# First transfers of a persistent LoRA kernel on two queues: SyncE's list reordered, ScalarE issues some transfers, TensorE multiplies zeros first

## The reference

```
w = weights[conditions]                       # [64, 128, 128]
x = x + einsum('bct,bcd->bdt', x, w)          # first layer
H = einsum('btd,od->bto', x, W)               # W is 1024 x 1024
xa = einsum('btd,brd->btr', x, A[adapter])    # rank 16
delta = einsum('btr,bor->bto', xa, B[adapter]) * s[adapter]
out = x + H + delta                           # second layer
```

## Time and profile before

| | us |
|---|---|
| median of 3 runs | 772.71 (772.51 to 773.09) |
| the profiled execution | 773.48 |
| its span, first to last instruction | 771.7 |
| outside the span | 1.8 |
| PE busy / DVE busy / ACT busy / POOL busy | 760.3 / 613.8 / 503.9 / 190.1 |

### The profile page before, as it was taken

One profiled execution on the slowest core, in us unless ns is written; L12 is line 12 of the kernel. 1 busy time (PEld: TensorE's weight loads), 2 busy tenths in 40 slices (PEclk: granted clock), 3 DMA queues, 4 the chain that ended last, 5 costly groups with the idle time before them and its releaser, 6 DMA issues.

```text
span 771.7 us, 16748 instructions
## 1 busy us (share of the span) xinstructions
PE 760.3 (99%) x4418; PEld 719.3 (93%) x4418; DVE 613.8 (80%) x1386; ACT 503.9 (65%) x1173; POOL 190.1 (25%) x428
## 2 busy tenths in 40 slices
PE   7999999999999999999999999999999999999998
PEld 4567999999999999999999999999999999999997
DVE  5999977788777788777788777788777788777774
ACT  3476666676666676666676666676666676666673
POOL 2733202233212333202332212323212232212200
PEclk9999999999999999999999999999999999999999
DMA  8433343432343432333432343432343432343222
GB/s 288 169 131 116 124 144 123 151 120 90 122 143 122 150 117 94 122 143 122 150 118 92 122 143 122 150 112 98 122 143 122 150 117 94 122 143 122 89 90 83
DMA packets 47291, 98.32 MB, mean 127 GB/s; under 512 B 6438, under 2 KB 25894, under 8 KB 47270
## 3 DMA queue, kind: packets, MB, share of 16 engines
q1 hardware_dynamic: 47266, 98.08, 37.4%
q10 hardware_dynamic: 4, 0.00, 0.0%
HBM read 63.45 MB, written 34.60 MB: 127 GB/s over the span
## 4 chain that ended last, share of the span: by engine, by line
PE 87%; DVE 3%; DMA 1%; issue 1%; ACT 0%; SPq 0%; DVEq 0%; ACTq 0%
PE bank L1381 73%; PE o_ps L1442 4%; PE bank L1420 3%; PE o_ps L1441 3%; PE o_ps L1443 3%; DMA out<-o_sb 1%; DVE c_sb L892 1%; DVE w_lo L889 1%; DVE z_lo L889 0%; DVE x_lo L889 0%; PE bank L1425 0%; PE o_ps L1432 0%; DVE x_raw L889 0%; ACT x_hi L510 0%; ACT z_hi L510 0%
## 5 line engine op out<-in xcount | busy, mean ns | idle before, releaser
L1381 PE MATMUL bank<-w_hi,x_hi 128*128 128x342 f32 (+2 forms) x1200 | 390.5, 325 | 0.7 <-ACT c_sb L510 0.6
L1381 PE MATMUL bank<-w_lo,x_hi 128*128 128x342 f32 (+2 forms) x1200 | 387.1, 323 | 0.0
L1381 PE MATMUL bank<-w_hi,x_lo 128*128 128x342 f32 (+2 forms) x1200 | 386.5, 322 | 0.0
L1381 PEld LDWEIGHTS bank<-w_hi,x_hi 128*128 128x128 f32 x1200 | 225.8, 188 | 9.8 <-ACT c_sb L510 2.1
L1381 PEld LDWEIGHTS bank<-w_lo,x_hi 128*128 128x128 f32 x1200 | 225.6, 188 | 2.8
L1381 PEld LDWEIGHTS bank<-w_hi,x_lo 128*128 128x128 f32 x1200 | 226.1, 188 | 0.0
L889 DVE TENSOR_TENSOR x_lo<-x_raw,x_hi 128x256 fp32r<-128x256 f32 (+1 forms) x270 | 145.5, 547 | 32.0 <-ACT x_hi L510 27.3
L510 ACT ACTIVATE x_hi<-x_raw 128x256 fp32r<-128x256 f32 (+1 forms) x270 | 133.7, 507 | 52.5 <-PE bank L1381 45.7
L303 POOL TENSOR_TENSOR w_lo<-a_ride,w_hi 128x160 fp32r<-128x160 f32 x30 | 15.6, 519 | 507.0 <-ACT w_hi L510 507.0
L510 ACT ACTIVATE c_sb<-bank 128x342 f32<-128x342 f32 x190 | 85.7, 452 | 41.0 <-PE bank L1381 38.6
L510 ACT ACTIVATE z_hi<-c_sb 128x340 fp32r<-128x340 f32 (+1 forms) x128 | 60.4, 490 | 54.8 <-DVE c_sb L892 54.8
(11 more groups left out here) (104 smaller groups left out, 878.2 us busy)
## 6 DMA issues: line engine op xcount, KB each, us to landing
x_raw<-xT SPq DMA_DIRECT2D x62, 512.0 KB, 4.9
out<-o_sb SPq DMA_DIRECT2D x62, 512.0 KB, 2.7
b_stack_raw<-b_split SPq DMA_DIRECT2D x128, 128.0 KB, 2.4
a_now<-lora_a SPq DMA_DIRECT2D x64, 64.0 KB, 3.4
c_raw<-cond_w SPq DMA_DIRECT2D x64, 64.0 KB, 1.8
w_lo_raw<-wB SPq DMA_DIRECT2D x7, 342.0 KB, 7.5
w_hi_raw<-wB SPq DMA_DIRECT2D x5, 342.0 KB, 6.0
x_raw<-xT SPq DMA_DIRECT2D x4, 256.0 KB, 4.7
```

The costliest lines, as they stand in the source:

```text
L1381: last = nc.tensor.matmul(bank[:, lo:hi], x[:, left, c * C:(c + 1) * C], w[:, c, FIRST[o]:FIRST[o] + WIDTH[o]], start=opens and c == 0 and ...
```

## The change

On ACT's queue, ahead of the adapter numbers and the scales, stand now the two first halves of x of pair 0; SP's queue begins with `b12`, and the second halves of x come later in it. ACT, and no longer SP, reads the adapter numbers of pair 0 and starts its two A transfers, behind its first rounding (`hi_of("17")`). In SP's list the condition matrices of pair 0 (`load_c(0, 0, 0)`, with its wait and its two register reads) move ahead of the two saves of `b_split`, and the stack of pair 0 (`load_b(0, 0, 0)`, behind the wait for the saves) moves ahead of A of pair 1 (`load_a(sp, 0, 0, 1)`). TensorE gets 9 + 4 matmuls of zeros, 128 columns each, around the matmul of the scales; nothing reads their result. `load_a`, `load_x_half` and `adapters` become functions of the engine that issues.

```
+            load_x_half(act, 0, 0, x_half_landed[0])
+            load_x_half(act, 1, 0, x_half_landed[1])
             act.dma_start(adapter_sb[:, :], adapter_idx).then_inc(adapter_landed, 16)
             act.dma_start(s_row[:, :], scalings).then_inc(s_landed, 16)
...
             hi_of("17", w_block("b12"))
+            act.wait_ge(adapter_landed, 16)
+            load_a(act, 0, 0, 0)
...
-            load_x_half(0, 0, x_half_landed[0])
             load_w(sp, "b12")
-            load_x_half(1, 0, x_half_landed[1])
             load_w(sp, "b01")
-            load_x_half(0, 1, x_landed[0][0])
-            load_x_half(1, 1, x_landed[0][1])
             load_w(sp, "b30")
+            load_x_half(sp, 0, 1, x_landed[0][0])
             load_w(sp, "b21")
-            sp.wait_ge(adapter_landed, 16)
-            load_a(0, 0, 0)
+            load_x_half(sp, 1, 1, x_landed[0][1])
             load_w(sp, "b20")
...
             load_x(0, 0, 1, 1)
+            sp.wait_ge(cond_landed, 16)
+            load_c(0, 0, 0)
             sp.wait_ge(b_hi_ready, 1)
             save_b(0, z_hi[0])
+            sp.wait_ge(adapter_landed, 16)
             sp.wait_ge(b_lo_ready, 1)
             save_b(1, z_lo[0])
-            sp.wait_ge(first_scaled, 8)
-            load_a(0, 0, 1)
-            sp.wait_ge(cond_landed, 16)
-            load_c(0, 0, 0)
             sp.wait_ge(b_saved, 32)
             load_b(0, 0, 0)
+            sp.wait_ge(first_scaled, 8)
+            load_a(sp, 0, 0, 1)
             step(0, 0)
...
+            pe.wait_ge(zeros_ready, 1)
+            for _ in range(9):
+                nc.tensor.matmul(o_ps[1][:, 0:P], xa_cols[0][:, :], xa_cols[0][:, :], start=True, stop=True)
+
             pe.wait_ge(s_landed, 16)
             pe.wait_ge(ones_ready, 1)
             nc.tensor.matmul(o_ps[0][:, 0:NAD], ones[0:1, :], s_row[0:1, :], start=True, stop=True).then_inc(s_spread, 1)
+            for _ in range(4):
+                nc.tensor.matmul(o_ps[1][:, 0:P], xa_cols[0][:, :], xa_cols[0][:, :], start=True, stop=True)
             dense("b12")
```

More of the change, by code:

```diff
@@ L307, in o_last, with load_x_half @@
             return x_raw[0][:, n, 2 * h:2 * h + 2, :].rearrange("p k c -> p (k c)")
+        def load_x_half(eng, n, h, landed_sem):
+            eng.dma_start(x_raw[0][:, n, 2 * h:2 * h + 2, :].rearrange("p k c -> p (k c)"),
+                          xT[n, :, h * (KC // 2):(h + 1) * (KC // 2), :].rearrange("p k c -> p (k c)"))\
+               .then_inc(landed_sem, 16)
         def load_w(eng, b):
@@ L311, in load_w, with adapters, load_a @@
             eng.dma_start(w_block(b), wB[k, j, :, :, :]).then_inc(w_landed[b], 16)
+        def adapters(eng, i, j, d):
+            b = i * 4 + 2 * (j + d)
+            return [eng.value_load(adapter_sb[0:1, bass.ds(b + n, 1)], min_val=0, max_val=NAD - 1) for n in range(2)]
+        def load_a(eng, i, j, d):
+            found = adapters(eng, i, j, d)
+            after(eng, a_summed, i, j, d - 1, 4)
+            for n in range(2):
+                eng.dma_start(a_now[:, n, :, :].rearrange("p k r -> p (k r)"),
+                              lora_a[bass.ds(found[n], 1), :, :, :].rearrange("a p k r -> (a p) (k r)"))\
+                   .then_inc(a_landed, 16)
         @block.sync
@@ L319, in load_x @@
                              xT[bass.ds(b, 1), :, :, :].rearrange("b p k c -> (b p) (k c)")).then_inc(x_landed[s][n], 16)
[L321 to L331, removed]
             def load_b(i, j, d):
-                found = adapters(i, j, d)
+                found = adapters(sp, i, j, d)
                 after(sp, lora_done["00"], i, j, d - 1)
@@ L370, in step @@
                 if exists(i, j, 2):
-                    load_a(i, j, 2)
+                    load_a(sp, i, j, 2)
                 if exists(i, j, -1):
@@ L416, in _ @@
             store(0, 1, -1, 1)
-            load_a(0, 1, 2)
+            load_a(sp, 0, 1, 2)
             store(0, 1, -1, 0)
```

## The result

The changed kernel takes 776.56 us (median of 7 runs, 775.72 to 782.54). The kernel before, beside it on the same chip, takes 773.09 (772.51 to 773.37, 7 runs). The ratio is 1.0058, 95% interval 1.0040 to 1.0075: slower by 3.5 us. The forecast was 776.8, range 773.2 to 780.2.

The account below looks back on a forecast made before the run. The prediction took TensorE, busy 760.3 of 771.7 us, as the bound, with losses nearly all before pair 2. A 5.4 us lateness from the rides less 1.3 won back gave +4.1, 776.8 us, range 773.2 to 780.2.

Parts of the forecast that it names:

- Zeros first: TensorE's start: zero matmuls delay `b12` but at the higher clock; gain 0.4 to loss 1.9 us, hidden, counted 0.
- Two queues: Start of the weight stream: fuller DMA engines bring the weights 0.7 us sooner (bounds 0 and 1.5), by itself no time.
- A of pair 0: ScalarE's issue of A: landed at 13, hidden by POOL's later wait of 4.39 us; counted 0, at most 0.5.
- The saves: SP's saves of `b_split` behind the condition numbers: reached at 24.4, saved at 31.3 against 29.6 before; bounds 28.1 and 33.
- the bound of 7.7 us: Late bound for the condition numbers' landing: 7.7 us from issue, as x of pair 1 behind them took, giving 22.9.
- late bound of 33: Latest time at which the saves of `b_split` would be done and SP go on, against the 31.3 taken.
- The stack: Stack of pair 0 behind the saves: ready at 37.8 against 36.07, TensorE 1.7 us late at the adapter matmuls.
- The rides: POOL's copies for product "5" of pair 1: A landed at 39.2, ready 6.9 us later at 46.1, TensorE 5.4 us late.
- The rival of the clock: TensorE's clock falls in the wait before product "5": 2.3 us more, 779.1 us; chance 0.21.
- The 1.3 us won back: TensorE's two later waits, 0.7 and 0.6 us, would absorb 1.3 us of its lateness.
- The sum: Whole kernel: 5.4 us of lateness less 1.3 won back, +4.1 us, median from 772.71 to 776.8.

Follow-up runs that it names:

- no_zeros: saves_as_before without the 9 + 4 matmuls of zeros; 773.62 us, ratio 1.0001 to the kernel before.
- saves_as_before: The changed kernel with the tail of SP's list (saves, A of pair 1, condition matrices, stack) in the order of before; 773.42 us, ratio 1.0003.
- a_early_saves_late: The changed kernel with A of pair 1 fetched ahead of the wait for the saves, the saves still behind the condition matrices; 776.83 us, ratio 1.0053.
- store_first: saves_as_before with the store of the second sample moved ahead of the next x in each step; 772.02 us, ratio 0.9985.
- busy_in_the_wait: The changed kernel with nine 128-column float32 matmuls that nothing reads ahead of the wait for `b_stack`; 776.36 us, ratio 1.0042.
- saves_early_a_late: The changed kernel with the condition matrices put behind the saves again, A of pair 1 still last; 773.62 us, ratio 1.0000.
- again: The changed kernel measured and profiled once more, with no edit; 777.91 us, ratio 1.0052.

## Why the prediction came out near, step by step

**Zeros first: right in effect, late in time.** Forecast for `b12`: start 7.5 to 8.3, end 9.9 to 10.7. It started at 8.57 and the next block at 11.76, 3.19 us later and not 2.4. In four of the nine profiles with zeros it came as forecast: start at 7.7 to 7.9, 2.47 us for the 8 halves; in the other five they took 3.3 to 4.5. Worth nothing either way, as no_zeros shows (4.20 us for the 8 halves, the same time), because A of pair 0 takes the gain.

**Two queues: the start was undersized.** Forecast: 0.7 us sooner. SP issued the condition numbers at 11.55, 3.6 us before the 15.19 of the earlier trace rows: two halves of x, the wait for the adapter numbers, two reads and two issues of A had also left SP's list, which the prediction did not follow down the queue. For pairs 0 and 1 that gave "5" 1.1 us sooner (saves_as_before), and in the end nothing.

**A of pair 0: 14.5 and not 13, and not hidden.** In the nine profiles in which ScalarE issues it, TensorE waits for its scaling in five, 0.5 to 2.5 us at about 16 us: in the four in which the first block took 2.47 us, and in no_zeros. In the other four, in which the zeros had left that block slow, there is none. Either way the next block with 358 columns starts at 20.9 to 21.6 (saves_as_before 20.91, the changed kernel 21.17), but for 22.7 in a_early_saves_late and 24.1 in store_first. So the two terms, each put at nothing, hide each other.

**The saves: two errors that cancel.** SP came to them at 21.9 and not at 24.4, but went on at 31.6, as forecast (31.3). From the first issue to SP's next step it took 9.7 us where 6.9 were allowed. The prediction priced the saves at 205 GB/s from their first moment; that is what they reach in the end, not at the start. Before, behind x of pair 1, the stretches from 23 to 27 read 205 to 238 GB/s; why the start is slow here, no run shows:

```profile
24.00:25.00 1.00, 1.00 (x5) 0.64 (x4) 1.00 (x3) 0.42 (x1) 0.59 (x1) 1.00 0.45 49
...
27.00:28.00 1.00, 1.00 (x5) 0.61 (x4) 1.00 (x3) 1.00 (x2) 0.00 (x0) 1.00 0.50 205
```

The order of landing is as the bound of 7.7 us had it. The Trainium skill ("DMA: Bandwidth & Descriptors", section "Queues, rings and completion order") says that a semaphore's increment lands behind the earlier writes; 7.9 us for 256 bytes agrees. The DMA share is near half in both rows. The same page, section "Why a DMA increments its semaphore by 16 and not by 1", says that as many of the 16 engines are used as divide the slowest dimension; it is 8 here, and 0.50 agrees. (The prediction's late bound of 33 for this term is not the sum of the terms that it names: 22.9, 1.33, 0.86, 5.1 and 1.8 make 32.0.)

**The stack: right.** Forecast 1.7 us late at the adapter matmuls; 2.2 by the timeline (38.37 against 36.21). This, which the prediction counted as part of a longer wait, is the main loss: "5" starts at 42.67 in busy_in_the_wait, 2.0 late, with nothing else against it.

**The rides: the step that failed.** "POOL began the rides of pair 1 at 30.19 when A landed and ended its second copy at 37.07, 6.9 us" was carried over as the price, and with it "the rides are ready at 46.1". A landed at 38.7, near the forecast of 39.2; the copies ended at 42.5. No wait for them is in any profile. One instruction of the chain, in the trace of before:

```profile
34.53 0.76 POOL L299 TENSOR_TENSOR a_ride<-a_now,a_ride 128x32 f32<-128x32 f32 x1
```

In the changed kernel it is the row at 41.56: 0.25 us. Before, VectorE worked through that microsecond (1.00 in the stretch from 34 to 35) on L1152, with two tiles in SBUF as operands; in the changed kernel it had stopped at 41.4, since it too waited for TensorE. In saves_early_a_late the chain slows and quickens within one execution: the last of its 5.7 us fall in VectorE's pause from 37.8 to 39.3, and L299 takes 0.25 there. A busy VectorE alone is not what counts: in the trace of before L299 takes 0.25 us again at 73.04, beside VectorE's `z_lo<-bank,z_hi`, which reads one operand from a bank of PSUM, and 0.81 at 189.76 beside its `x_lo<-x_raw,x_hi`, two tiles in SBUF. The Trainium skill ("GPSIMD Engine Reference", section "2. Architecture") says that GpSimd reads and writes SBUF through ports that it shares with VectorE; the rows agree, though no run here stops VectorE and nothing else. The prediction's own bounds for this term, 6.6 to 7.5, came from one execution with VectorE at work, though it had written that VectorE's splits would wait behind TensorE. Over the profiles the chain takes 3.7 to 8.3 us (8.2 in saves_as_before).

**The rival of the clock: it occurs, at another wait.** It was given 0.21 and 2.3 us. The fall comes behind the wait for `b_stack`, of 2.3 to 4.7 us, in part of the executions, and costs 1.6 us to "5" in again and 3.2 in the profile of the changed kernel (44.27 and 45.82 against 42.67). In the profiles it goes with the length of the wait: every one of 2.3 to 4.7 us has a fall with it, none of 1.4 us or less has. The profile of the changed kernel shows a second one at 99 us:

```profile
85.72 7.73 DMA out<-o_sb
...
101.40 0.85 PE bank L1421 x3
```

```profile
100.00:101.00 1.00, 1.00 (x5) 1.00 (x5) 1.00 (x4) 0.52 (x2) 0.78 (x4) 0.50 0.00 0
```

The store took 7.73 us where the earlier trace rows have 5.87, TensorE waited 2.5 us for what hangs on it, and fell to half speed again. The Trainium skill ("TensorE: Matmul & The Clock Gate", section "HAM oscillation — how this bites in real kernels") says that a wait for a transfer brings the clock down; the granted clock here agrees.

**The 1.3 us won back: wrong.** The two later waits stayed (0.7 and 0.6 in again) or grew. They end with work of VectorE and a store that hang on the same late pair (the store was issued at 80.63 before and at 85.72 in the changed kernel, 5.1 us later, as "5" is), so the whole chain moved with TensorE. A wait can only be won back if what ends it does not move; store_first shows what it takes.

**The sum.** Forecast: 5.4 - 1.3 = 4.1. By the runs: 2.0 for the stack, about 2 for the clock in those executions in which it falls, nothing for the rides, nothing back. The median of 776.56 is itself one of the four runs at full clock, 775.72 to 776.56 or 2.6 to 3.5 us above the 773.09 of before, so that 0.6 to 1.5 us of it stay open beside the 2.0. Why the clock falls in one execution and not in the next is not settled either: the runs without a profile show their mean clock and not their waits.

## What to carry to other kernels

When a transfer is moved behind a wait, follow everything that hangs on its queue position, and price it from an empty queue as well as from a full one. A duration on an engine belongs to the state of its neighbours: if the change makes VectorE idle or gives it other work, GpSimd's times from before are not the price. And an idle time of TensorE like those of 2.3 to 4.7 us here is to be counted with a fall of its clock as a second price, which work that nothing reads can take away. Last, a total inside the range shows nothing of the path: here a wait of 5.4 us that did not come was replaced by others of about the same sum.

## What the runs showed of the hardware

- GpSimd's addition of 128 x 32 float32 took 0.76 and 0.81 us beside a VectorE instruction with two tiles in SBUF as operands, 0.25 beside an idle VectorE, and 0.25 beside one that read an operand from PSUM.
- TensorE's granted clock fell to half in or right behind every profiled wait of 2.3 to 4.7 us and behind none of 0.7 to 1.4 us once it had worked at the higher level, and stayed there for some 3 to 6 us of work; the mean over the whole execution moved only from 1.000 to 0.993 to 0.998.
- 18 halves of zeros (4.21 us), then a wait of 0.76 us and more work, did not give the first real block the higher level throughout: 3.35 us for 8 halves, where block `b22` takes 2.46 at the full clock (busy_in_the_wait). Over nine profiles with zeros the first block took 2.47 us in four and 3.3 to 4.5 in five.
- The scales' 32 bytes were there at 3.2 to 3.3 us when they were second on ScalarE's queue, and at 5.9 to 6.6 behind two transfers of 256 KB.
